# A decoder layer on one core: another order of work in the rows of the first two batches

## The chip, the cores and the metric

The kernel runs on one core of a Trainium2 chip. The time is the device time of one execution in microseconds. The kernel before was run three times: 654.48 us is the median, 654.33 the lowest and 656.54 the highest. One more execution was profiled, and every row below is from it.

## The reference

The layer works on 32 batches of 112 rows of 256 numbers (float32), one batch independent of the next:

```
x = x + attention(layernorm(x), wq, wk, wv, wo)     # 8 heads of 128, rms norm and rotation of q and k, causal softmax
x = x + gelu(layernorm(x) @ ctx^T) @ ctx            # ctx: 375 rows of 256 for each batch
x = x + ffn(layernorm(x), w1, b1, w2, b2)           # 256 -> 1024 -> 256, weights, biases and inputs rounded to fixed point
```

wq, wk, wv and wo are 256 x 1024 in size (1 MB each), w1 and w2 are 1024 x 256 (1 MB each).

## The kernel before, in words

**Precision.** The attention's matrix products run on float16 pairs: a number is rounded to a high half, and the rest goes into a low half. Each product is three matmuls (high x high, high x low, low x high). So xn (the normalised x), q, k, o and the four attention weights are all "rounded" by the Scalar engine (ACT, high half) and then "split" by the Vector engine (DVE, low half = value - high half). The weights are first lifted by a power of two that follows from the sum of their squares: ACT squares, TensorE (PE) sums over partitions (`sum_weights`), DVE bounds the sum (`bound_weights`, L435), GpSimd (POOL) takes the root (`root_weights`, L334), DVE makes the power of two (`lift_weights`, L440), ACT rounds with it as scale, DVE splits.

**Pipeline.** Each engine runs a list of its own: `body(i)` for i from -3 to 36, and in one body it works on different stages of several batches. The order within a body is written out by hand, engine by engine, and semaphores tie the engines together. There is no loop in the hardware: all bodies are unrolled. "The row of batch j" is here the DVE body in which c = j: it begins with `turn_cos_k(j)` (L425: k times cosines, out of PSUM) and `turn_sin_k(j)` (L433), goes on with the sums of squares of k and q (`sum_squares_k` L565, `sum_squares_q` L602), the rotation of q (`turn_cos_q` L568, `turn_sin_q` L605, `turn_q` L612), and ends with `split_k(j)` (L637); `split_q(j)` (L520) is in the body after it. ACT's part of a row is: scale and round k (L769 to L784), round q (L786 to L798), normalise and round o of the batch before, then square k, copy v, square q of the batch after. POOL adds the two halves of k's rotation (`turn_k`, L352) and takes the rms roots (L356, L375).

**One buffer each.** xn16, xT16 (its transposed copy), the q, k and v banks of PSUM, turn_c, turn_s and qk16 have one buffer. So the transposition of batch j's xn (`transpose_x`, a DMA that SP issues, L285) waits for the last v matmul of batch j - 1.

**The start.** Batch 0's xn is made first. Then `prepare_projections` lifts, rounds and splits wk, wq and wv (DVE L468, ACT L721). PE projects k, q and v of batch 0, and between k and q it sums wo's squares. On DVE the row of batch 0 then runs: the statistics of batch 1's x (`stats_x`), then `prepare_wo` (L481): bound, lift and split wo, and only then `turn_cos_k(0)`. Batch 1's x is normalised in the middle of this row, behind `turn_cos_q(0)`, and split behind that. On ACT, `prepare_wo` (L730) squares wo, waits for its lift, rounds it, and then `square_k(0)` follows, which `turn_cos_k(0)` waits for. In the next DVE body, behind `split_q(0)`, stand `clip_weights` of w1 and w2 and `fixed_biases` (L486, L492): they wait for ACT's `round_weights` (L738), which stands between the v copies and `square_q(1)`.

**Queues.** SP issues every DMA in the order of its list: `transpose_x(1)`, then the load of batch 2's x, of w1 and w2 (`load_weights`, L244; they go into the place of the raw projection weights), then the transpositions of k and q of batch 0.

Of the kernel before, what the change touches and what calls it, by code (L numbers as in the profile page):

```python
# [77 lines left out]
def decoder_layer(nc, x, ctx_rows, ctx_cols, wq, wk, wv, wo, w1_cols, b1, w2_cols, b2, tables, out):  # L78
# [15 lines left out]
    with ExitStack() as stack:  # L94
# [225 lines left out]
        @block.gpsimd  # L320
        def _(pool):
            pool.memset(ones_pp[:, :], 1.0).then_inc(const_done, 1)
            pool.memset(nhalf[:, :], -0.5).then_inc(const_done, 1)
            pool.memset(ln_eps[:, :], LN_EPS).then_inc(const_done, 1)
            pool.memset(eps_0[:, :], RMS_EPS / QK_LIFT ** 2).then_inc(const_done, 1)
            pool.memset(v_sb[:, :, D:VW], V_DROP).then_inc(const_done, 1)
            pool.memset(pool_cell[:, :], 0.0).then_inc(const_done, 1)
            pool.wait_ge(const_done, 6)

            def carry_wait():  # L330

                pool.tensor_tensor(pool_cell[:, :], pool_cell[:, :], pool_cell[:, :], ALU.mult)

            def root_weights():  # L334
                for n in TURN:
                    pool.wait_ge(w_sq_done, TURN.index(n) + 1)
                    pool.tensor_tensor(w_root[:, n:n + 1], w_sq[:, n:n + 1], nhalf[:, 0:1], ALU.pow).then_inc(w_root_done, 1)

            def variance_x(j):
                pool.wait_ge(x_stats_done, done(j))  # L340
                pool.tensor_tensor(ve[0][:, :], mv[0][:, 1:2], ln_eps[:, :], ALU.add).then_inc(x_var_done, 1)  # L341

            def add_b2(j):
                if j.has(1):
                    pool.wait_ge(out_done, done(j.plus(-1)))
                pool.tensor_tensor(x3b[:, :], x3[:, :], b2_rows[:, :], ALU.add).then_inc(x3b_done, 1)  # L346

            def root_x(j):
                pool.wait_ge(x_var_done, done(j))
                pool.tensor_tensor(rstd[0][:, :], ve[0][:, :], nhalf[0:T, 0:1], ALU.pow).then_inc(x_rstd_done, 1)  # L350

            def turn_k(j):  # L352
                pool.wait_ge(k_sin_done, done(j))
                pool.tensor_tensor(turn_c[:, 1, :], turn_c[:, 1, :], turn_s[:, 1, :], ALU.add).then_inc(k_turned, 1)  # L354

            def rms_root_k(j):  # L356
                pool.wait_ge(k_summed, done(j))
                if is_first(j):
                    pool.wait_ge(eps_done, TURN.index(1) + 1)
                pool.tensor_tensor(ms[:, 1, :], ss[:, 1, :], rms_eps[:, 1, :], ALU.add).then_inc(k_ms_done, 1)  # L360
                pool.wait_ge(k_ms_done, done(j))
                pool.tensor_tensor(rms[:, 1, :], ms[:, 1, :], nhalf[0:T, 0:H], ALU.pow).then_inc(k_rms_done, 1)  # L362

            def mask_later_keys(j):
                pool.wait_ge(exp_done, done(j))
                carry_wait()
                p = p_sb.rearrange("k (h t) -> k h t", h=H)
                pool.affine_select(out=p, in_=p, compare_op=ALU.is_ge, fill=0.0, base=0,  # L368
                                   pattern=[[0, H], [1, T]], channel_multiplier=-1).then_inc(p_done, 1)

            def root_x3(j):
                pool.wait_ge(x3_stats_done, done(j))
                pool.tensor_tensor(rstd[2][:, :], ve[2][:, :], nhalf[0:T, 0:1], ALU.pow).then_inc(x3_rstd_done, 1)

            def rms_root_q(j):  # L375
                pool.wait_ge(q_summed, done(j))
                if is_first(j):
                    pool.wait_ge(eps_done, TURN.index(0) + 1)
                pool.tensor_tensor(ms[:, 0, :], ss[:, 0, :], rms_eps[:, 0, :], ALU.add).then_inc(q_ms_done, 1)
                pool.wait_ge(q_ms_done, done(j))  # L380
                pool.tensor_tensor(rms[:, 0, :], ms[:, 0, :], nhalf[0:T, 0:H], ALU.pow).then_inc(q_rms_done, 1)  # L381

            def root_x2(j):
                pool.wait_ge(x2_stats_done, done(j))
                pool.tensor_tensor(ve[1][:, :], mv[1][:, 1:2], ln_eps[:, :], ALU.add).then_inc(x2_var_done, 1)  # L385
                pool.wait_ge(x2_var_done, done(j))
                pool.tensor_tensor(rstd[1][:, :], ve[1][:, :], nhalf[0:T, 0:1], ALU.pow).then_inc(x2_rstd_done, 1)

            def body(i):
                a, b, c, d, f, g = (Batch(i + 3), Batch(i + 2), Batch(i + 1), Batch(i - 0), Batch(i - 2), Batch(i - 3))  # L390
                if a.inside(B):
                    variance_x(a)
                if g.inside(B):
                    add_b2(g)
                if a.inside(B):
                    root_x(a)
                    if a.off == 0:
                        root_weights()
                if b.inside(B):
                    turn_k(b)  # L400
                    rms_root_k(b)
                if c.inside(B):
                    mask_later_keys(c)
                if f.inside(B):
                    root_x3(f)
                if b.inside(B):
                    rms_root_q(b)
                if d.inside(B):
                    root_x2(d)

            for i in range(-3, B + 5):
                body(i)
# [3 lines left out]
        def _(dve):  # L416
# [51 lines left out]
            def prepare_projections():  # L468
                one, two, three = TURN[0:3]
                bound_weights(one)  # L470
                bound_weights(two)
                lift_weights(one)
                lift_weights(two)
                split_projection(one)
                bound_weights(three)
                lift_weights(three)
                split_projection(two)
                split_projection(three)
                dve.wait_ge(table_in, 32)

            def prepare_wo():  # L481
                bound_weights(3)
                lift_weights(3)
                split_wo()

            def clip_weights(n):  # L486

# [153 lines left out]
            def body(i):  # L641
# [4 lines left out]
                    stats_x2(f)  # L646
                if d.inside(B):
                    split_q(d)
                    if d.off == 0:
                        clip_weights(0)  # L650
                        clip_weights(1)
                        fixed_biases()
                if f.inside(B):
                    normalise_x2(f)
                if b.inside(B):
                    stats_x(b)
                if i.inside(B):
                    residual_out(i)
                if e.inside(B):
                    split_o(e)  # L660
                if c.inside(B):
                    if c.off == 0:
                        prepare_wo()
                    turn_cos_k(c)
                    turn_sin_k(c)
                if g.inside(B):
                    residual_ctx(g)
                if c.inside(B):
                    sum_squares_k(c)
                    turn_cos_q(c)  # L670
                if b.inside(B):
                    normalise_x(b)
                if g.inside(B):
                    stats_x3(g)
# [1 line left out]
                    gelu_inner(f)  # L676
                if h.inside(B):
                    clip_hidden1(h)
                if b.inside(B):
                    split_xn(b)  # L680
                    if b.off == 0:
                        prepare_projections()
# [13 lines left out]
                if e.inside(B):  # L696
                    residual_attention(e)
                if c.inside(B):
                    split_k(c)

            for i in range(-3, B + 5):
# [4 lines left out]
        def _(act):  # L706
# [20 lines left out]
                round_projection(two)  # L727
                round_projection(three)

            def prepare_wo():  # L730
                act.wait_ge(wo_in, 16)
                for c in range(MC):
                    act.activation(wo16[:, 0, c * HH:(c + 1) * HH, :].bitcast(BF16), wo_raw[:, c * HH:(c + 1) * HH, :], ACT.Square,
                                   scale=W_PEAK, accum_out=w_sum[:, 3, c:c + 1]).then_inc(w_squared, 1)
                act.wait_ge(w_lift_done, 4)
                act.activation(wo16[:, 0, :, :], wo_raw[:, :, :], ACT.Copy, scale=w_lift[:, 3:4]).then_inc(wo_done, 1)

# [108 lines left out]
            def body(i):  # L846
# [2 lines left out]
                    square_h(g)  # L849
                if i.inside(B):  # L850
                    relu0(i)
                if c.inside(B):
                    round_xn(c)
                    if c.off == 0:
                        prepare_projections()
# [13 lines left out]
                    round_o(e)  # L869
                if c.inside(B):  # L870
                    if c.off == 0:
                        prepare_wo()
                    square_k(c)
                if d.inside(B):
                    copy_v1(d)
                    copy_v0(d)
# [2 lines left out]
                        round_weights(1)  # L879
                if c.inside(B):  # L880
                    square_q(c)
                if f.inside(B):
                    copy_xn2T(f)
                if h.inside(B):
# [7 lines left out]
        def _(pe):  # L892
# [47 lines left out]

            def project_k(j):
                pe.wait_ge(xT_landed, landed_once(j))
                if j.has(3):
                    pe.wait_ge(x2_done, done(j.plus(-3)))
                project(1, 0, k_ps[:, 0, :], j)
# [188 lines left out]
```

## Time and profile before

| what | value |
|---|---|
| median of three runs | 654.48 us |
| the profiled execution | 654.7 us, its span 652.9 us |
| DVE busy | 588.1 us (90%) |
| PE busy | 593.3 us (91%) |
| ACT busy | 543.0 us (83%) |
| POOL busy | 348.0 us (53%) |
| mean granted clock of TensorE | 0.974 of full speed |

The span is what the trace covers; the execution's own time is 1.8 us more. Matmuls overlap in the pipeline, so PE's busy time is not a measure of how full PE is. In the chain of work that ended last, 75% of the span is DVE.

### The profile page before, as it was taken

Reading aid. Unit: us, or ns where it says so; the run is one execution under the profiler, and the core shown is the slowest. Engines: PE = TensorE matmul, PEld = TensorE weight load, DVE = VectorE, ACT = ScalarE, POOL = GpSimd, SP = SyncE. Lnnn points to the kernel's source line nnn. Section 1 sums busy time; section 2 is a strip of 40 time slices with the busy share of each in tenths; the row PEclk is TensorE's granted clock in tenths of the full one; section 3 lists DMA queues with packets and bytes.
Section 4 is the critical chain, followed back from the end, with each engine's and each line's share of the span. In section 5 each row is a group of like instructions: output and inputs, shape, how many; then the busy total and the mean of one; then the engine's idle time right before and its main releaser. Section 6 shows DMA issues by size and latency. Waiting matters only on the chain.

```text
span 652.9 us, 13103 instructions
## 1 busy us (share of the span) xinstructions
PE 593.3 (91%) x4624; PEld 477.3 (73%) x4624; DVE 588.1 (90%) x1339; ACT 543.0 (83%) x1402; POOL 348.0 (53%) x430
## 2 busy tenths in 40 slices
PE   1746889999999999999999999999999999997864
PEld 1424667777887788888778877888887788776753
DVE  3768899999999999999999999999999999998442
ACT  6675788999999999989998899999889999998522
POOL 1134555665555565666655555656666555556111
PEclk9967999999999999999999999999999999999978
DMA  8071566766776766667687676666677777666451
GB/s 296 0 200 36 114 139 138 137 138 150 149 148 137 147 133 142 141 141 153 133 151 152 143 152 138 137 142 132 143 149 138 150 152 146 134 141 138 89 109 37
DMA packets 222641, 88.92 MB, mean 136 GB/s; under 512 B 200704, under 2 KB 217552, under 8 KB 222320
## 3 DMA queue, kind: packets, MB, share of 16 engines
q1 hardware_dynamic: 222576, 88.08, 63.6%
q8 instruction: 37, 0.61, 0.4%
q14 instruction: 28, 0.23, 0.1%
HBM read 34.84 MB, written 3.67 MB: 59 GB/s over the span
## 4 chain that ended last, share of the span: by engine, by line
DVE 75%; ACT 9%; PE 5%; POOL 3%; issue 3%; DMA 3%; SPq 0%; ACTq 0%; DVEq 0%
DVE turn_s L433 11%; DVE turn_c L425 8%; DVE qk L524 8%; DVE o L550 5%; DVE ss L566 5%; DVE turn_c L614 5%; DVE ss L603 5%; DVE qk L639 4%; DVE h_t L590 2%; DVE y_out L545 2%; DVE g L628 2%; DVE x L634 2%; DVE stat L534 1%; POOL turn_c L354 1%; DVE xn L600 1%
## 5 line engine op out<-in xcount | busy, mean ns | idle before, releaser
L912 PE MATMUL psum<-wqkv,xT 128*112 128x512 f16 x384 | 148.3, 386 | 12.5 <-DMA xT<-xn 9.1
L913 PE MATMUL psum<-wqkv,xT 128*112 128x512 f16 x384 | 147.4, 384 | 0.0
L914 PE MATMUL psum<-wqkv,xT 128*112 128x512 f16 x384 | 147.1, 383 | 0.0
L354 POOL TENSOR_TENSOR turn_c<-turn_c,turn_s 112x1024 f32<-112x1024 f32 x32 | 75.7, 2365 | 48.4 <-DVE turn_s L433 48.4
L912 PEld LDWEIGHTS psum<-wqkv,xT 128*112 128x112 f16 x384 | 50.7, 132 | 43.4 <-DMA xT<-xn 9.7
L425 DVE TENSOR_TENSOR turn_c<-psum,cos_t 112x1024 f32<-112x1024 f32 x64 | 77.8, 1215 | 0.0
L433 DVE TENSOR_TENSOR turn_s<-psum,sin_t 112x1024 f32<-112x1024 f32 x64 | 77.7, 1214 | 0.0
L914 PEld LDWEIGHTS psum<-wqkv,xT 128*112 128x112 f16 x384 | 50.7, 132 | 34.1 <-issue 1.9
L922 PE MATMUL psum<-wo,oT 128*112 128x256 f16 x256 | 71.0, 277 | 4.7 <-DMA oT<-o 3.5
L524 DVE SCALAR_TENSOR_TENSOR qk<-turn_c,rms,qk 112x128 f16<-112x128 f32 x256 | 69.2, 343 | 2.6 <-ACT qk L796 2.5
L924 PE MATMUL psum<-wo,oT 128*112 128x256 f16 x256 | 71.0, 277 | 0.0
L923 PE MATMUL psum<-wo,oT 128*112 128x256 f16 x256 | 71.0, 277 | 0.0
L913 PEld LDWEIGHTS psum<-wqkv,xT 128*112 128x112 f16 x384 | 50.7, 132 | 27.6 <-issue 1.3
L385 POOL TENSOR_TENSOR ve<-mv,ln_eps 112x1 f32<-112x1 f32 x32 | 6.6, 205 | 109.1 <-DVE mv L518 109.1
L1051 PE MATMUL psum<-v_sb,p_sb 112*112 112x129 f32 x512 | 62.1, 273 | 0.5 <-DVE turn_s L433 0.5
L1051 PEld LDWEIGHTS psum<-v_sb,p_sb 112*112 112x112 f32 x512 | 58.9, 176 | 0.9 <-POOL p_sb L368 0.9
L346 POOL TENSOR_TENSOR x3b<-x,b_rows 112x256 f32<-112x256 f32 x32 | 48.3, 1509 | 16.5 <-DVE y_out L545 13.2
L362 POOL TENSOR_TENSOR rms<-ms,nhalf 112x8 f32<-112x8 f32 x32 | 55.1, 1723 | 2.5
L381 POOL TENSOR_TENSOR rms<-ms,nhalf 112x8 f32<-112x8 f32 x32 | 53.3, 1665 | 2.5
L341 POOL TENSOR_TENSOR ve<-mv,ln_eps 112x1 f32<-112x1 f32 x32 | 9.2, 287 | 81.0 <-DVE mv L537 81.0
L1013 PE MATMUL psum<-qkT 128*112 128x112 f16 x256 | 42.6, 218 | 10.0 <-DVE turn_s L433 9.7
L961 PE MATMUL psum<-ctx_in,g 125*112 125x256 f32 x192 | 48.6, 390 | 3.3 <-ACT v_sb L708 3.3
(107 smaller groups left out, 1699.2 us busy)
## 6 DMA issues: line engine op xcount, KB each, us to landing
ctxT<-in_ctx_cols SPq DMA_DIRECT2D x32, 375.0 KB, 3.4
ctx_in<-in_ctx_rows SPq DMA_DIRECT2D x32, 375.0 KB
x_in<-in_x SPq DMA_DIRECT2D x32, 112.0 KB, 2.3
out_y<-y_out SPq DMA_DIRECT2D x32, 112.0 KB, 2.9
w_raw<-in_w SPq DMA_DIRECT2D x2, 1024.0 KB, 6.1
w_raw<-in_wk SPq DMA_DIRECT2D x2, 512.0 KB, 5.0
w_raw<-in_wq SPq DMA_DIRECT2D x2, 512.0 KB, 6.5
w_raw<-in_wv SPq DMA_DIRECT2D x2, 512.0 KB, 8.2
```

What stands on the lines that cost most here:

```text
L354: pool.tensor_tensor(turn_c[:, 1, :], turn_c[:, 1, :], turn_s[:, 1, :], ALU.add).then_inc(k_turned, 1)
L362: pool.tensor_tensor(rms[:, 1, :], ms[:, 1, :], nhalf[0:T, 0:H], ALU.pow).then_inc(k_rms_done, 1)
L425: return dve.tensor_tensor(turn_c[:, w, :].rearrange("t (b h d) -> t b h d", b=2, d=D), ps.rearrange("t b (h d) -> t b h d", d=D), cos_t[: ...
L433: return dve.tensor_tensor(turn_s[:, w, :].rearrange("t (h two f) -> t h two f", two=2, f=HALF), halves, table, ALU.mult)
L524: last = dve.scalar_tensor_tensor(out=qk16[:, 0, 1, at], in0=turn_c[:, 0, at], scalar=rms[:, 0, h:h + 1], in1=qk16[:, 0, 0, at], op0=ALU.m ...
L912: pe.matmul(dst, hi, wqkv[:, 0, c, w, cols], start=c == 0, stop=False)
L913: pe.matmul(dst, hi, wqkv[:, 1, c, w, cols], start=False, stop=False)
L914: last = pe.matmul(dst, lo, wqkv[:, 0, c, w, cols], start=False, stop=c == MC - 1)
L922: pe.matmul(y_ps, oT16[:, h, :], wo16[:, 0, h, :], start=first and h == heads[0], stop=False)
L923: pe.matmul(y_ps, oT16[:, h, :], wo16[:, 1, h, :], start=False, stop=False)
L924: product = pe.matmul(y_ps, oT16[:, H + h, :], wo16[:, 0, h, :], start=False, stop=last and h == heads[-1])
L1051: last = pe.matmul(o_ps[:, h // OH, at:at + VW], p_sb[:, h * T:(h + 1) * T], v_sb[:, h, :], start=h % OH == 0, stop=h % OH == OH - 1 or h ...
```

## The change

The change moves instructions and adds one wait; no instruction's size or number changes.

- Batch 1's x: `stats_x(1)` goes behind the first split of `prepare_projections`, `normalise_x(1)` to its end; `split_xn(1)` goes behind `turn_sin_k(0)`. POOL's `variance_x(1)` and `root_x(1)` go between the second and the third of the weight roots. ACT's `round_xn(1)` goes behind `square_k(0)`.
- wo: DVE's `bound_weights(3)` goes to the end of `prepare_projections`, `lift_weights(3)` between `turn_cos_k(0)` and `turn_sin_k(0)`, and `split_wo` ahead of `split_k(0)`. ACT's rounding of wo goes behind `square_q(0)`.
- The feed-forward weights: `clip_weights` of w1 and w2 and `fixed_biases` go from behind `split_q(0)` to ahead of `split_k(1)`.
- PE's `project_k(1)` waits for `turn_sin_k(0)` by itself, since xn's order no longer implies it.

```diff
@@ POOL @@
             def body(i):
+                early = a.off == 1
-                if a.inside(B):
+                if a.inside(B) and not early:
                     variance_x(a)
...
-                if a.inside(B):
+                if a.inside(B) and not early:
                     root_x(a)
                     if a.off == 0:
-                        root_weights()
+                        root_weights(TURN[0:2])
+                        variance_x(Batch(1))
+                        root_x(Batch(1))
+                        root_weights(TURN[2:])
...
@@ DVE, prepare_projections @@
                 lift_weights(two)
                 split_projection(one)
+                stats_x(Batch(1))
                 bound_weights(three)
                 lift_weights(three)
                 split_projection(two)
                 split_projection(three)
+                normalise_x(Batch(1))
+                bound_weights(3)
                 dve.wait_ge(table_in, 32)
-
-            def prepare_wo():
-                bound_weights(3)
-                lift_weights(3)
-                split_wo()
...
@@ DVE, body @@
                 if d.inside(B):
                     split_q(d)
-                    if d.off == 0:
-                        clip_weights(0)
-                        clip_weights(1)
-                        fixed_biases()
...
-                if b.inside(B):
+                if b.inside(B) and b.off != 1:
                     stats_x(b)
...
                 if c.inside(B):
+                    turn_cos_k(c)
                     if c.off == 0:
-                        prepare_wo()
-                    turn_cos_k(c)
+                        lift_weights(3)
                     turn_sin_k(c)
+                    if c.off == 0:
+                        split_xn(Batch(1))
...
-                if b.inside(B):
+                if b.inside(B) and b.off != 1:
                     normalise_x(b)
...
-                if b.inside(B):
+                if b.inside(B) and b.off != 1:
                     split_xn(b)
...
                 if c.inside(B):
+                    if c.off == 0:
+                        split_wo()
+                    if c.off == 1:
+                        clip_weights(0)
+                        clip_weights(1)
+                        fixed_biases()
                     split_k(c)
...
@@ ACT @@
-            def prepare_wo():
+            def square_wo():
                 act.wait_ge(wo_in, 16)
...
+            def round_wo():
                 act.wait_ge(w_lift_done, 4)
...
-                if c.inside(B):
+                if c.inside(B) and c.off != 1:
                     round_xn(c)
...
                     if c.off == 0:
-                        prepare_wo()
+                        square_wo()
                     square_k(c)
+                    if c.off == 0:
+                        round_xn(Batch(1))
...
                     square_q(c)
+                    if c.off == 0:
+                        round_wo()
...
@@ PE @@
             def project_k(j):
                 pe.wait_ge(xT_landed, landed_once(j))
+                if j.off == 1:
+                    pe.wait_ge(k_sin_done, done(j.plus(-1)))
```

## Rows read from the trace of the kernel before

**Rows 1.** Busy us in one stretch: PE, PEld, DVE, ACT, POOL; PEclk, DMA share, GB/s
```profile
101.70:585.00 483.30, 482.40 (x3864) 391.84 (x3863) 478.62 (x1102) 437.48 (x1154) 291.35 (x351) 1.00 0.69 143
```

**Rows 2.** The chain that ended last: start us, us, what
```profile
24.95 2.01 ACT wo L736
27.06 2.35 DVE wo L461
...
35.50 2.37 DMA xT<-xn
```

**Rows 3.** Timeline of DVE to 51 us: start, us, line, operation [idle before <-releaser]
```profile
17.62 0.16 DVE L438 TENSOR_SCALAR w_sq<-psum 128x1 f32<-128x1 f32 x1 [1.77 <-PE psum L902]
...
23.42 0.42 DVE L534 BATCH_NORM_STATS2 stat<-x_in 112x6 f32<-112x256 f32 x1
...
29.65 1.21 DVE L425 TENSOR_TENSOR turn_c<-psum,cos_t 112x1024 f32<-112x1024 f32 x1
30.77 1.22 DVE L433 TENSOR_TENSOR turn_s<-psum,sin_t 112x1024 f32<-112x1024 f32 x1
...
37.77 1.23 DVE L614 TENSOR_TENSOR turn_c<-turn_c,turn_s 112x1024 f32<-112x1024 f32 x1
...
42.30 2.19 DVE L524 SCALAR_TENSOR_TENSOR qk<-turn_c,rms,qk 112x128 f16<-112x128 f32 x8 [1.11 <-ACT qk L796]
...
48.60 0.69 DVE L418 TENSOR_SCALAR w2T<-w_int 128x2048 bf16<-128x2048 int16 x1 [1.10 <-ACT w_int L741]
...
50.28 0.42 DVE L534 BATCH_NORM_STATS2 stat<-x_in 112x6 f32<-112x256 f32 x1
...
50.84 1.19 DVE L425 TENSOR_TENSOR turn_c<-psum,cos_t 112x1024 f32<-112x1024 f32 x1
```

**Rows 4.** Timeline of ACT, 22 to 64 us
```profile
22.71 0.19 ACT L733 ACTIVATION_READ_ACCUMULATOR wo<-wo_raw 128x1 f32 x1
...
42.97 1.02 ACT L819 ACTIVATE sq<-psum 112x1024 f32<-112x1024 f32 x1 [0.70 <-PE psum L914]
...
44.85 3.72 ACT L741 ACTIVATE w_int<-w_raw 128x2048 int16<-128x2048 f32 x2
48.45 1.03 ACT L830 ACTIVATE sq<-psum 112x1024 f32<-112x1024 f32 x1
...
57.57 1.28 ACT L772 ACTIVATE kn<-turn_c,rms 112x128 f32<-112x128 f32 x4 [0.57 <-POOL rms L362]
...
63.35 1.10 ACT L803 ACTIVATE on<-psum,rden 112x128 f32<-112x128 f32 x4
```

**Rows 5.** Timeline of PE, 23 to 39 us
```profile
23.04 0.58 PE L902 MATMUL psum<-w_sum,ones_pp 128*128 128x1 f32 x4 [0.59 <-ACT wo L733]
...
28.46 0.38 PE L914 MATMUL psum<-wqkv,xT 128*112 128x512 f16 x1
37.91 0.68 PE L912 MATMUL psum<-wqkv,xT 128*112 128x512 f16 x1 [9.07 <-DMA xT<-xn]
```

**Rows 6.** Timeline of POOL, 36 to 39 us
```profile
36.97 1.65 POOL L381 TENSOR_TENSOR rms<-ms,nhalf 112x8 f32<-112x8 f32 x1
```

**Rows 7.** Issues of line L236 (the load of batch 1's x): issue time and landing
```profile
L236 SPq DMA_DIRECT2D x_in<-in_x x1: 484/484/484, 4.4 to 4.4; - x1
...
DMA to landing us min/median/max: 8.8/8.8/8.8
```

**Rows 8.** Timeline of DVE in batch 1's row, 54 to 68 us
```profile
54.20 1.22 DVE L425 TENSOR_TENSOR turn_c<-psum,cos_t 112x1024 f32<-112x1024 f32 x1
...
61.13 1.23 DVE L639 TENSOR_TENSOR qk<-kn,qk 112x1024 f16<-112x1024 f32 x1 [0.96 <-ACT qk L708]
62.28 0.23 DVE L509 RECIPROCAL rden<-psum 112x6 f32<-112x6 f32 x2
...
67.76 1.21 DVE L425 TENSOR_TENSOR turn_c<-psum,cos_t 112x1024 f32<-112x1024 f32 x1
```

**Rows 9.** Issues of line L275 (q's transposition) to 50 us: time to landing
```profile
DMA to landing us min/median/max: 4.7/4.7/4.7
```

More of the change, by code:

```diff
@@ L332, in carry_wait, with root_weights @@
                 pool.tensor_tensor(pool_cell[:, :], pool_cell[:, :], pool_cell[:, :], ALU.mult)
-            def root_weights():
-                for n in TURN:
+            def root_weights(turns):
+                for n in turns:
                     pool.wait_ge(w_sq_done, TURN.index(n) + 1)
```

## The prediction

> **What bounds the kernel now.** I read the busy time by stretch first. From 102 to 585 us the DVE is busy for 478.62 of 483.30 us [rows 1], 99%, and there each batch costs what its DVE work costs. Nothing in that stretch is edited. So I looked for when the stretch can begin, with the chain of waits: at the start the chain runs through ACT's rounding of wo (24.95, 2.01 us), DVE's split of wo (27.06, 2.35 us), and later through the transposition of batch 1's xn (35.50, 2.37 us) [rows 2]. All three stand in the row of batch 0, and all are moved. The timelines of the engines then give the dates: the reader is to see that `turn_cos_k` of batch 0 starts at 29.65, of batch 1 at 50.84 [rows 3], of batch 2 at 67.76 [rows 8]. If batch 2's start comes earlier by some time, everything behind it (same order, same waits, each on something in these rows or later) comes earlier by the same time. So the sum is made for this one date, 67.76, and subtracted from the end.
>
> The trace is of an execution of 654.7 us with a span of 652.9; the median of the runs is 654.48, 0.2 lower.
>
> **Batch 1's statistics, at no cost.** `stats_x(1)` takes 50.84 - 50.28 = 0.56 us [rows 3]. It goes ahead of the third weight bound, before which DVE idles 1.77 us, from 15.85 to 17.62, waiting for PE [rows 3]. x of batch 1 is there by 4.4 + 8.8 = 13.2 (or half a us more, if the landing counts from the issue's end) [rows 7]. POOL's two small operations behind it fit ahead of the third root too, since 1.2 us of that idle time are left. If the cover were gone, 0.56 us would push the v weights and through them only the v projection, which is late for nothing here.
>
> **Start of batch 0's row: 29.65 becomes 24.0.** PE was done with k of batch 0 at 23.04 - 0.59 = 22.45, for it waited that long for ACT's squares of wo [rows 5]. ACT ends these squares at 22.71 + 0.19 = 22.90 [rows 4] as before, and `square_k(0)`, now next, takes 1.02 [rows 4]: 23.92. On DVE, `normalise_x(1)` takes the place of the statistics at 23.42 (some 0.42, until 23.85); the sum of wo's squares is there at 23.04 + 0.58 = 23.62 [rows 5], and the bound takes 0.16. So `turn_cos_k(0)` starts at 24.0, earlier by 5.65.
>
> **The lift inside the rotation: 0.2.** ACT began to round wo at 24.95 [rows 2], right behind the lift, so the root was there by 24.8, and its bound is no later now; DVE gets to the lift at 24.0 + 1.12 = 25.12 and does not wait. One operation like the bound and the wait for its own result: 0.2. `turn_sin_k(0)` starts at 25.3, before at 30.77 [rows 3].
>
> **To `split_q(0)`: 42.30 becomes 36.85.** Between `turn_sin_k(0)` and `split_q(0)` lay 42.30 - 30.77 = 11.53 us, and the latter waited for ACT (1.11 idle) [rows 3]: POOL's rotation and roots, ACT's scaling and rounding. None of that chain is edited, so 25.3 + 11.53 = 36.85, if nothing else is late:
> - DVE: the six operations from `turn_sin_k(0)` to `turn_q(0)` take 1.12 each (30.77 - 29.65), `split_xn(1)` 0.4: done at 32.5. (Before, 8.23 from 30.77 to the end of `turn_q` at 37.77 + 1.23 [rows 3], with the normalising and splitting of xn and a wait in it; by that figure 33.5.) `split_wo` with its two small followers took 29.65 - 27.06 = 2.6 [rows 2, 3]: 35.1 (36.1). Then `split_k(0)`, one step of 1.15 (62.28 - 61.13 [rows 8]): 36.25 (37.25). So it hides, or costs 0.4 by the other figure. I take 0.
> - ACT: q of batch 0 is projected by about 26.3 (PE finishes the v behind it at 28.46 + 0.38 = 28.84 [rows 5], 24 matmuls later); `round_xn(1)` and `square_q(0)` follow, then the rounding of wo (2.01) until some 29.3. k's scaling is wanted at about 31, so the rounding is in ACT's idle time and wo is there long before `split_wo`.
>
> **The transposition of xn(1): off the path.** The low half is done at about 26.9, so what holds it is the last v matmul at 28.84: it starts there, not at 35.50, and lands at 31.2 where PE started k of batch 1 at 37.91 [rows 5]. In the trace k took from there to 42.97 - 0.02 (ACT waited 0.70 for it [rows 4]), 5.0 us, with the first matmul 0.68 us long and the last of batch 0's 0.38 [rows 5]. With the same 5.0, k is there at 36.3, and ACT is free for `square_k(1)` at 36.8. The added wait of `project_k(1)` is over at 26.5, before the transposition lands; what queues behind it on PE (q, scores, v) is not held by it.
>
> **Start of batch 1's row: 50.84 becomes 39.5.** Behind `split_q(0)` (some 2.1 to the next instruction's start) stood the clips and biases until 50.28 [rows 3]: 50.28 - 42.30 - 2.1 = 5.9 us, mostly waits for ACT's rounding of w1 and w2. They leave. 36.85 + 2.1 + 0.56 = 39.5, a gain of 11.3. x of batch 2 and the squares of k (36.8 + 1.02) are there.
>
> **Inside batch 1's row: 0.9 is given back.** ACT's piece from `square_k(1)` (42.97) to the end of `square_q(1)` (48.45 + 1.03), with the rounding of w1 and w2 in it, takes 6.5 [rows 4]. It now runs from 36.8 to 43.3. DVE is ready for `turn_cos_q(1)` at 39.5 + 3 x 1.12 = 42.85, so it waits 0.45. w1 and w2 land in time: their loads stand behind the transposition, which moves by 6.6; ACT took them without a wait at 44.85 and in the middle of 3.72 [rows 4], so they are there by 38.2 and 40.1, and are wanted at 38.7 and 40.5.
> From `turn_cos_q(1)` to where DVE had nothing left took 61.13 - 0.96 - 54.20 = 5.97 [rows 8]: 49.3. Now the clips and biases: the second clip and the biases took 50.28 - 48.60 = 1.68 [rows 3], another clip 0.6: 2.3, until 51.6. `split_k(1)`, which k's rounding would allow at 39.5 + 1.12 + 61.13 - 50.84 - 1.12 = 49.8, starts at 51.6; the reciprocals of the softmax sums follow 1.15 later and take 0.23 [rows 8]: 53.0. They release ACT's normalising of o, which by its own queue could start at 39.5 + 63.35 - 50.84 = 52.0. So the clips hold it by 1.0. From there to `turn_cos_k(2)` it was 67.76 - 63.35 = 4.41 [rows 4, 8]: 57.4.
>
> **Sum.** 67.76 - 57.4 = 10.4. 654.7 - 10.4 = 644.3; against the median 644.1, which I take. Between 11.3 and 10.4 lies what batch 1's row gives back.
>
> One place where a rule speaks against the change: in the trace POOL's power for q's rms runs from 36.97 for 1.65 us [rows 6], and DVE's `turn_q`, with two inputs in SBUF, runs in it at 37.77 with its usual 1.23 [rows 3]: neither is held up. The Trainium skill says otherwise (SBUF — State Buffer, "Who interferes with whom"): a DVE instruction with two SBUF inputs and a POOL instruction that reads SBUF lock each other out for a whole instruction. By that rule `split_xn(1)`, which now starts as POOL's rotation of k does, would hold POOL or be held; rival C has the sum.
>
> **Rivals.**
> A. The forecast, 60%: 643.3 to 645.2 by the roundings of the steps.
> B. Row 1 gives back more, 17%. The scores of batch 0 stand behind q's transposition and behind `turn_sin_k(1)`, their exponentials ahead of k's scaling on ACT. Before, the latter wait ended last, at 50.84 + 1.12 + 1.22 = 53.2, 2.35 behind `turn_cos_k(1)`, and ACT still had 0.57 us idle ahead of the scaling [rows 4]. q's transposition landed 4.7 after its issue [rows 9]; from 39.05 that is 43.75 now, 4.25 behind `turn_cos_k(1)`. So the scaling would be 4.25 - 2.35 - 0.57 = 1.3 late, of which the clips' hold hides 1.0. Every us more goes through whole: a landing after twice 4.7 gives 5.0 in all, 649.1. For it: the 2 MB of w1 and w2 come in ahead on the same queue. Against: they come 2 us earlier, relative to the transposition, than before, so 4.7 should be the upper end.
> C. The lock, 6%. If POOL's rotation of k starts first, `split_xn(1)` waits its 2.4 us; k's sums come 1.45 late for the rms, `split_wo` ends at 37.5 and `split_k(0)` at 38.65, so `split_q(0)` is 1.8 late; the clips then weigh less, and `turn_cos_k(2)` comes at 58.8: 645.5. If DVE is first, 644.4.
> D. More gain, 7%: neither `square_q(1)` nor the clips hold the row, 11.7 in all: 642.8.
> E. Nothing at the end, 6%: the long stretch is held by something that these rows don't start (PE is as busy there as DVE, 482.40 of 483.30 [rows 1]). 654.5. Against it: PE's list, too, follows from the same rows.
> F. Slower, 4%: w1 lands so late that ACT's rounding, which stands ahead of `square_q(1)` and so ahead of all of batch 1's q, holds the row. It takes the whole gain away from 38.7 + 10.4 + 0.5 = 49.6 on, 21 us behind the transposition at 28.84, where it took at most 44.85 - 35.50 = 9.4; at 55 it would be 660. Against it: nothing but the transpositions shares the queue.
>
> **How the numbers follow.** 644.1 is A's time. 642.4 to 648.5 holds A, C, D and most of B, some 87%; what is left out is E, F and the tail of B, and some allowance for what I don't see. Faster by over 0.5% (3.3 us, about what can be told from no change) is A to D: 0.90. Within 0.5%: E, 0.06. Slower: F, 0.04.
>
> **What would show it.** In the trace after: `turn_cos_k(0)` at 24.0; the transposition of xn(1) right behind the last v matmul of batch 0, at 28.9; `split_q(0)` at 36.9; `turn_cos_k(1)` at 39.5 with no clip ahead of it; DVE waiting 0.4 for ACT's `square_q` ahead of `turn_cos_q(1)`; `split_k(1)` right behind the biases, with no idle time; `turn_cos_k(2)` at 57.4; and from there every date 10.4 earlier. Wrong would be a wait of ACT for w1's load, DVE idle ahead of `split_wo`, a late k(1) on PE, or dates that drift back behind batch 2.

## The result, and the profile after

645.43 us, the median of four runs (643.96 to 648.09), against 654.40 for the kernel before on the same chip, now the median of four runs as well: a ratio of 0.986, 95% interval 0.984 to 0.9881. The forecast was 644.1, in a range of 642.4 to 648.5. Direction and mechanism came out, but one step of the sum failed. The profiled execution hides that at first sight: its span is 10.7 us shorter than before, but of these only 8.8 are there when the last batch's row starts.

The head of the page after:

```profile
span 642.2 us, 13103 instructions
PE 593.6 (92%) x4624; PEld 477.1 (74%) x4624; DVE 587.8 (92%) x1339; ACT 543.5 (85%) x1402; POOL 350.5 (55%) x430
```

DVE's timeline after (line numbers moved by 4: L429 is turn_cos, L437 turn_sin, L526 split_q, L422 a clip):

```profile
23.54 1.22 DVE L429 TENSOR_TENSOR turn_c<-psum,cos_t 112x1024 f32<-112x1024 f32 x1
...
24.86 1.23 DVE L437 TENSOR_TENSOR turn_s<-psum,sin_t 112x1024 f32<-112x1024 f32 x1
26.00 0.41 DVE L602 TENSOR_TENSOR xn<-xn 112x256 f16<-112x256 f32 x1
...
36.47 2.19 DVE L526 SCALAR_TENSOR_TENSOR qk<-turn_c,rms,qk 112x128 f16<-112x128 f32 x8 [0.58 <-ACT qk L804]
...
39.14 1.19 DVE L429 TENSOR_TENSOR turn_c<-psum,cos_t 112x1024 f32<-112x1024 f32 x1
...
42.85 1.23 DVE L429 TENSOR_TENSOR turn_c<-psum,cos_t 112x1024 f32<-112x1024 f32 x1 [0.27 <-ACT sq L838]
...
47.60 1.47 DVE L616 TENSOR_TENSOR turn_c<-turn_c,turn_s 112x1024 f32<-112x1024 f32 x1
48.99 0.68 DVE L422 TENSOR_SCALAR w1T<-w_int 128x2048 bf16<-128x2048 int16 x1
49.59 0.68 DVE L422 TENSOR_SCALAR w2T<-w_int 128x2048 bf16<-128x2048 int16 x1
...
51.28 1.22 DVE L641 TENSOR_TENSOR qk<-kn,qk 112x1024 f16<-112x1024 f32 x1
52.41 0.23 DVE L511 RECIPROCAL rden<-psum 112x6 f32<-112x6 f32 x2
54.63 2.19 DVE L526 SCALAR_TENSOR_TENSOR qk<-turn_c,rms,qk 112x128 f16<-112x128 f32 x8 [1.98 <-ACT qk L804]
...
58.91 1.21 DVE L429 TENSOR_TENSOR turn_c<-psum,cos_t 112x1024 f32<-112x1024 f32 x1
```

The reader is to see three things. The rows of the first two batches start as forecast: 23.54 (24.0), 39.14 (39.5), against 29.65 and 50.84 [rows 3]; this execution began its weights 0.37 earlier, and with that added the second date is 39.51. The clips run in one go behind `turn_q(1)`. But behind the reciprocals stands a wait of 1.98 for ACT that the forecast did not have, and batch 2's row starts at 58.91 (59.28 with the 0.37 added), not 57.4.

PE after: the first matmul of k of batch 1, the first of the scores of batch 0:

```profile
30.98 0.42 PE L924 MATMUL psum<-wqkv,xT 128*112 128x512 f16 x1 [2.50 <-DMA xT<-xn]
...
43.34 0.34 PE L1027 MATMUL psum<-qkT 128*112 128x112 f16 x1 [5.29 <-DMA qkT<-qk]
```

k of batch 1 starts at 30.98 instead of 37.91 [rows 5]. The scores now wait for q's transposition, 4.6 us from issue to landing, as rival B had it, and no longer for `turn_sin_k(1)`.

POOL and ACT after, in batch 1's row, tell where the 1.98 comes from:

```profile
47.00 0.98 POOL L368 TENSOR_SCALAR_AFFINE_SELECT p_sb<-p_sb 112x896 f32<-112x896 f32 x1
47.96 2.38 POOL L379 TENSOR_TENSOR ms<-ss,rms_eps 112x8 f32<-112x8 f32 x1
50.42 1.64 POOL L381 TENSOR_TENSOR rms<-ms,nhalf 112x8 f32<-112x8 f32 x1
```

```profile
49.15 1.06 ACT L714 ACTIVATE qk<-kn 112x1024 f16<-112x1024 f32 x1
52.15 1.28 ACT L798 ACTIVATE qk<-turn_c,rms 112x128 f16<-112x128 f32 x4 [1.95 <-POOL rms L381]
53.33 1.26 ACT L804 ACTIVATE qk<-turn_c,rms 112x128 f16<-112x128 f32 x4
54.50 1.11 ACT L811 ACTIVATE on<-psum,rden 112x128 f32<-112x128 f32 x4
```

The addition ahead of q's roots, 8 numbers a row, took 2.38 us; in the kernel before, the same instruction took 0.194 on the mean, and in batch 1's row:

```profile
58.60 0.19 POOL L379 TENSOR_TENSOR ms<-ss,rms_eps 112x8 f32<-112x8 f32 x1
```

In the changed kernel it ends at 50.34, just when DVE's second clip does (49.59 + 0.68 = 50.27). The roots, ACT's rounding of q, `split_q(1)` and the normalising of o follow it, each late. And DVE's `turn_q`, 1.47 us instead of 1.23, ends late beside the mask (47.00 to 47.98).

### The profile page after: what moved, and what is told of

Its sections match the earlier page's. It is cut to its first block, busy times and chain, and to the rows that moved or that the text cites. A ratio compares the mean times of both kernels' runs of the same rounds, so it can differ in the third digit from the quotient of the medians.

```text
span 642.2 us, 13103 instructions
## 1 busy us (share of the span) xinstructions
PE 593.6 (92%) x4624; PEld 477.1 (74%) x4624; DVE 587.8 (92%) x1339; ACT 543.5 (85%) x1402; POOL 350.5 (55%) x430
## 4 chain that ended last, share of the span: by engine, by line
DVE 74%; ACT 8%; PE 6%; issue 4%; POOL 4%; DMA 3%; SPq 0%; ACTq 0%; POOLq 0%
DVE turn_s L437 10%; DVE qk L526 9%; DVE turn_c L429 8%; DVE o L552 5%; DVE turn_c L616 5%; DVE ss L605 5%; DVE ss L568 5%; DVE qk L641 4%; DVE h_t L592 2%; DVE y_out L547 2%; DVE g L630 2%; DVE x L636 2%; DVE stat L583 1%; DVE xn L602 1%; DVE x L565 1%
## 5 line engine op out<-in xcount | busy, mean ns | idle before, releaser
L429 DVE TENSOR_TENSOR turn_c<-psum,cos_t 112x1024 f32<-112x1024 f32 x64 | 77.8, 1215 | 0.3 <-ACT sq L838 0.3
L437 DVE TENSOR_TENSOR turn_s<-psum,sin_t 112x1024 f32<-112x1024 f32 x64 | 77.7, 1215 | 0.0
L526 DVE SCALAR_TENSOR_TENSOR qk<-turn_c,rms,qk 112x128 f16<-112x128 f32 x256 | 69.1, 343 | 2.7 <-ACT qk L804 2.7
L1015 PE MATMUL psum<-xn2T,ctxT 128*125 128x112 f32 x384 | 48.8, 277 | 1.7 <-ACT xn2T L714 1.6
L975 PE MATMUL psum<-ctx_in,g 125*112 125x256 f32 x192 | 46.8, 380 | 3.3 <-ACT v_sb L714 3.3
```

The costliest lines, as they stand in the source:

```text
L429: return dve.tensor_tensor(turn_c[:, w, :].rearrange("t (b h d) -> t b h d", b=2, d=D), ps.rearrange("t b (h d) -> t b h d", d=D), cos_t[: ...
L437: return dve.tensor_tensor(turn_s[:, w, :].rearrange("t (h two f) -> t h two f", two=2, f=HALF), halves, table, ALU.mult)
L526: last = dve.scalar_tensor_tensor(out=qk16[:, 0, 1, at], in0=turn_c[:, 0, at], scalar=rms[:, 0, h:h + 1], in1=qk16[:, 0, 0, at], op0=ALU.m ...
```

## The experiments

Dates of different executions are compared from DVE's first split of wk on (12.6 to 13.5 us into the span). In the table: `turn_sin_k` of batches 1, 2, 4 and 31 so counted, and what is left from the last of these to the end of the span.

| kernel | k(1) | k(2) | k(4) | k(31) | rest |
|---|---|---|---|---|---|
| before | 38.58 | 55.52 | 89.40 | 573.10 | 66.4 |
| changed | 27.24 | 47.05 | 81.33 | 564.66 | 64.5 |
| changed, again | 27.25 | 47.65 | 81.52 | 564.75 | 67.0 |
| undo_wo | 32.68 | 52.41 | 86.66 | 570.12 | 66.5 |
| undo_clips | 32.28 | 49.22 | 83.07 | 566.15 | 66.6 |
| undo_xn | 27.86 | 46.46 | 80.77 | 563.90 | 67.6 |
| clips_in_row2 | 27.25 | 45.87 | 80.66 | 563.88 | 68.9 |
| clips_late_and_rounding_late | 27.26 | 45.84 | 80.61 | 563.83 | 65.1 |
| reduce_in_place_of_clips | 27.24 | 45.84 | 80.62 | 564.62 | 69.0 |
| mask_behind_q_roots | 27.24 | 45.97 | 80.28 | 563.35 | 65.2 |
| both_moved | 27.24 | 44.93 | 78.79 | 561.88 | 64.0 |

The forecast's date for k(2) was 57.4 + 1.12 - 13.37 = 45.2. The last column is the drain behind the last row; it goes from 64.0 to 69.0 over these executions. It makes up all of the 2.5 us between the two profiled spans of the changed kernel (642.2 and 644.7). So steps of 1 us are read from the dates, and the times are given beside them.

**The changed kernel again.** 

> The changed kernel once more, beside its variants. Theory (its gain is the earlier start of batch 2's row and nothing else): turn_cos_k(2) within 0.5 us of 58.9, every later row 8.4 to 8.9 ahead of the kernel before, and 8.5 to 9.5 us less in the median; what a single execution shows beyond that (10.7 in the profiled span) comes behind the last row and changes from run to run. Rival (the tail is shortened by the change): the span is 10 us or more shorter again, with 2 us of it behind the last row.

646.36 us (644.91 to 647.73) beside 654.06: ratio 0.9879 (0.9856 to 0.9901), 7.7 less, a little under what was expected. `turn_cos_k(2)` came at 59.46, 0.06 later than the latest that was expected, the last row 8.35 ahead on the common count, the rest of the span 67.0. The 2 us that the first profiled execution had won in the drain are not the change's. That k(2) is 0.6 later than in the first execution has a cause in these rows: q's transposition took 5.2 us to land, not 4.6, so the scores, the exponentials and POOL's mask came 0.6 later, and the mask (47.55 to 48.53) began together with `turn_q`:

```profile
47.54 2.07 DVE L616 TENSOR_TENSOR turn_c<-turn_c,turn_s 112x1024 f32<-112x1024 f32 x1
```

`turn_q` took 2.07 us where it took 1.47 in the first execution and takes 1.23 alone.

**Clips in batch 2's row.** 

> The clips and biases go from ahead of split_k(1) to batch 2's row, ahead of residual_attention(0), where DVE waited 1.45 us for PE. Theory L (in batch 1's row the two clips held GpSimd's addition for q's rms, 2.38 instead of 0.20 us, and through it ACT's rounding of q, 1.95 of wait, and split_q(1), 1.98 of wait): the addition takes 0.2 again, ACT rounds q right behind k, split_q(1) starts at 52.6, turn_cos_k(2) at 57.0 instead of 58.9. The clips' 2.3 us in batch 2's row cost 0 to 0.9, so rows from batch 4 on are 1.0 to 1.9 earlier, and the time 1 to 2 us less than the changed kernel's. Rival V (it is the clips' DVE time ahead of split_k(1), 2.3 us, not GpSimd): the same dates at batch 2, so this run alone does not part them; the next one does. Rival N (neither matters, q is late for another reason): turn_cos_k(2) stays at 58.9.

```diff
                     if c.off == 1:
-                        clip_weights(0)
-                        clip_weights(1)
-                        fixed_biases()
                     split_k(c)
...
+                if c.off == 2:
+                    clip_weights(0); clip_weights(1); fixed_biases()
                 if e.inside(B):
                     residual_attention(e)
```

Batch 2's row starts 1.2 to 1.8 earlier, and 0.5 to 0.9 of that is lost again by batch 4: 0.7 to 0.9 is left there, less than the 1.0 to 1.9 expected. 646.33 us (643.41 to 647.19), the same as the changed kernel's. POOL and then DVE in this run:

```profile
47.63 1.16 POOL L379 TENSOR_TENSOR ms<-ss,rms_eps 112x8 f32<-112x8 f32 x1
...
65.42 2.63 POOL L381 TENSOR_TENSOR rms<-ms,nhalf 112x8 f32<-112x8 f32 x1
```

```profile
47.23 1.51 DVE L616 TENSOR_TENSOR turn_c<-turn_c,turn_s 112x1024 f32<-112x1024 f32 x1
...
66.64 0.69 DVE L422 TENSOR_SCALAR w1T<-w_int 128x2048 bf16<-128x2048 int16 x1
67.24 0.69 DVE L422 TENSOR_SCALAR w2T<-w_int 128x2048 bf16<-128x2048 int16 x1
```

The addition is not back at 0.2: it still ends with `turn_q` (47.23 + 1.51 = 48.74), which has two inputs in SBUF. And in batch 2's row the clips now hold the end of POOL's roots: 2.63 instead of 1.64, until 68.05, where the clips end at 67.93. The expectation had missed both.

**Two row sums in place of the clips.** 

> As clips_in_row2, but in the old place of the clips stand two extra row sums over 112x1024 (2.25 us of DVE time, one input, results unused). Theory L (GpSimd was held by the kind of operation): GpSimd's addition stays at 0.2, ACT rounds q without the 1.95 wait; split_k(1) is as late as in the changed kernel (51.2), the softmax reciprocals release ACT at 52.9 and turn_cos_k(2) comes at 57.3. Rival V (DVE's time): turn_cos_k(2) at 58.9 as in the changed kernel.

```diff
                     if c.off == 1:
-                        clip_weights(0); clip_weights(1); fixed_biases()
+                        dve.tensor_reduce(spare[:, 0, :], heads(sq[:, 0, :]), AX_X, ALU.add)
+                        dve.tensor_reduce(spare[:, 1, :], heads(sq[:, 1, :]), AX_X, ALU.add)
                     split_k(c)
```

DVE and POOL:

```profile
48.85 1.21 DVE L707 TENSOR_REDUCE spare<-sq 112x8 f32<-112x1024 f32 x1
49.98 1.20 DVE L708 TENSOR_REDUCE spare<-sq 112x8 f32<-112x1024 f32 x1
51.11 1.21 DVE L642 TENSOR_TENSOR qk<-kn,qk 112x1024 f16<-112x1024 f32 x1
```

```profile
47.83 1.16 POOL L380 TENSOR_TENSOR ms<-ss,rms_eps 112x8 f32<-112x8 f32 x1
49.07 1.64 POOL L382 TENSOR_TENSOR rms<-ms,nhalf 112x8 f32<-112x8 f32 x1
```

DVE is as busy ahead of `split_k(1)` as with the clips, and k(2) stands at 45.84, as in clips_in_row2. The addition takes 1.16, not the 0.2 expected, for `turn_q` holds it here too. So behind a q that is late by that much, DVE's time ahead of `split_k(1)` doesn't hold the row, and rival V falls as the reason for the late row of the changed kernel: what the clips cost there they cost through POOL, 1.2 us (1.8 against the second execution). That this time of DVE is free in every case is not shown; undo_xn below has a case where it is not. This kernel was run once, 648.23 us, and nothing is read from that time.

**w1 and w2 rounded later as well.** 

> As clips_in_row2, and ACT rounds w1 and w2 behind square_q(1) instead of ahead of it. Theory: DVE's wait of 0.27 ahead of turn_cos_q(1) goes, square_q(1) starts at 38.2 instead of 41.8, and the 3.7 us of rounding end at 42.9, before ACT is wanted for xn of batch 2 (43.7): turn_cos_k(2) up to 0.3 earlier than in clips_in_row2, 56.7. Rival (q of batch 1 is not there at 38.2, or the exponentials are pushed): no gain or up to 0.5 lost.

```diff
-                    if d.off == 0:
-                        round_weights(0); round_weights(1)    # ahead of square_q(1)
...
                     square_q(c)
+                    if c.off == 1:
+                        round_weights(0); round_weights(1)
```

DVE's wait of 0.27 is gone, and k(2) is no earlier (45.84): k's scaling on ACT stands behind the exponentials, and these wait for the scores. No gain, no loss in the rows; 644.28 us (643.21 to 647.12), not parted from clips_in_row2.

**The parts undone one by one.** Each of the three is the reverse of one item of the change.

> The changed kernel with the clips and biases back behind split_q(0). Theory: w1 and w2 still come 6.6 us earlier than in the kernel before, so ACT has rounded them by 41.9; DVE waits for that and turn_cos_k(1) starts at 43.8 instead of 39.1; then batch 1's row runs unhindered, 16.9 long, and turn_cos_k(2) comes at 60.7 instead of 58.9: this part of the change is worth some 2 us, not the 5.9 that left batch 0's row. Rival (the wait for ACT's rounding was worth its whole 5.9): turn_cos_k(2) at 64 or later.

```diff
                     split_q(d)
+                    if d.off == 0:
+                        clip_weights(0); clip_weights(1); fixed_biases()
...
-                    if c.off == 1:
-                        clip_weights(0); clip_weights(1); fixed_biases()
                     split_k(c)
```

> The changed kernel with wo bounded, lifted, rounded and split ahead of turn_cos_k(0) as before. Theory (wo's preparation stood on the path): turn_cos_k(0) at 29.3 instead of 23.5, and all behind it 5.5 later, turn_cos_k(2) at 64.4, some 5.5 us more in the time. Rival (batch 0's row has slack, what counts is batch 1's xn): turn_cos_k(2) less than 2 us later.

```diff
+                    if c.off == 0:
+                        bound_weights(3); lift_weights(3); split_wo()
                     turn_cos_k(c)
-                    if c.off == 0:
-                        lift_weights(3)
...
                         square_wo()
+                        round_wo()
                     square_k(c)
```

> The changed kernel with batch 1's statistics, normalising, rounding and splitting back in batch 0's row (behind turn_cos_q(0)). Theory (off the path as soon as wo and the clips are moved): the transposition of xn(1) starts at 29.5 to 30 instead of 28.6, DVE waits 0.5 to 1 for ACT's half, turn_cos_k(1) at most 0.5 later, turn_cos_k(2) 0 to 0.5 later. Rival (the transposition of xn(1), which stood in the chain of waits before, is what the change gains by): batch 1's k comes late, and turn_cos_k(2) is over 2 us later.

```diff
-                stats_x(Batch(1))
-                normalise_x(Batch(1))
...
-                    if c.off == 0:
-                        split_xn(Batch(1))
...
-                if b.inside(B) and b.off != 1:
+                if b.inside(B):
                     stats_x(b)      # normalise_x, split_xn, POOL's and ACT's likewise
```

The first two came out near the dates expected. With the clips back, `turn_cos_k(1)` was at 43.83 and `turn_cos_k(2)` at 60.73, in an execution that began 0.35 earlier than the changed kernel's, so 0.4 late on the common count. With wo back, `turn_cos_k(2)` was at 64.75 in an execution that began 0.47 later, so 0.1 early. DVE with the clips back, then with wo back:

```profile
39.79 0.69 DVE L422 TENSOR_SCALAR w1T<-w_int 128x2048 bf16<-128x2048 int16 x1 [1.48 <-ACT w_int L749]
41.59 0.69 DVE L422 TENSOR_SCALAR w2T<-w_int 128x2048 bf16<-128x2048 int16 x1 [1.10 <-ACT w_int L749]
...
43.83 1.19 DVE L429 TENSOR_TENSOR turn_c<-psum,cos_t 112x1024 f32<-112x1024 f32 x1
```

```profile
27.08 2.35 DVE L465 SCALAR_TENSOR_TENSOR wo<-wo_raw,w_lift,wo 128x2048 f16<-128x2048 f32 x1 [2.14 <-ACT wo L743]
...
29.67 1.20 DVE L429 TENSOR_TENSOR turn_c<-psum,cos_t 112x1024 f32<-112x1024 f32 x1
```

wo's move is worth 5.3 us at k(4), the clips' 1.7. In time: 651.07 (649.58 to 651.91), ratio to before 0.9945 (0.9928 to 0.9962), and 646.97 (646.59 to 647.34), ratio 0.9888 (0.9864 to 0.9912); by the times alone the second is not parted from the changed kernel. xn's move, beside the other two, is worth less than nothing in this profile: without it k(1) comes 0.6 later, and k(2) 0.6 to 1.2 earlier, not 0 to 0.5 later; 646.30 us (646.03 to 647.70), not parted by time either. The three don't add up to the 8.1 us that the change wins at k(4) (5.3 + 1.7 - 0.6 = 6.4): the rest is won by more than one of them, and undoing one alone does not lose it. For undo_xn, POOL, DVE and ACT say why k(2) is earlier:

```profile
48.12 0.19 POOL L379 TENSOR_TENSOR ms<-ss,rms_eps 112x8 f32<-112x8 f32 x1
48.38 1.64 POOL L381 TENSOR_TENSOR rms<-ms,nhalf 112x8 f32<-112x8 f32 x1
```

```profile
44.14 1.22 DVE L426 TENSOR_TENSOR turn_c<-psum,cos_t 112x1024 f32<-112x1024 f32 x1 [1.12 <-ACT sq L831]
...
50.03 0.69 DVE L419 TENSOR_SCALAR w1T<-w_int 128x2048 bf16<-128x2048 int16 x1
```

```profile
53.71 1.14 ACT L804 ACTIVATE on<-psum,rden 112x128 f32<-112x128 f32 x4 [1.02 <-DVE rden L506]
```

DVE waits 1.12 for q's squares and comes to `turn_q` (48.89) and the clips that much later. The addition is over by then, 0.19 long; `turn_q` runs over the end of the roots, and neither is longer for it (1.23 and 1.64); the clips begin as the roots end (50.02). A stall that was removed had kept two engines apart. With q on time, ACT now waits 1.02 for the reciprocals, which stand behind the clips: here the clips do cost DVE's time.

**The mask behind q's roots.** 

> The changed kernel, where GpSimd masks batch 0's scores behind the two rms operations for batch 1's q, not ahead of them; clips and biases stay in batch 1's row. Theory L (an operation of GpSimd and one of DVE on the shared access hold each other only if they meet: the addition for q's rms met the clips because it stood behind the mask, which waits for the scores, and these for the transposition of q): the addition now runs at 46.5, ahead of turn_q and the clips, in 0.2; ACT rounds q right behind k; turn_q takes 1.23 again instead of 1.47. The mask meets turn_q and the clips instead and may be held up to 50.0, so the weighing of values ends by 53 and turn_cos_k(2) comes at 57.8 or earlier, against 58.9. Rival (whatever GpSimd runs there is held, and the row waits for it all the same): turn_cos_k(2) at 58.9 or later.

```diff
-                if c.inside(B):
+                if c.inside(B) and c.off != 0:
                     mask_later_keys(c)
...
                 if b.inside(B):
                     rms_root_q(b)
+                if c.off == 0:
+                    mask_later_keys(c)
```

POOL, then DVE:

```profile
46.76 0.20 POOL L379 TENSOR_TENSOR ms<-ss,rms_eps 112x8 f32<-112x8 f32 x1 [0.61 <-DVE ss L607]
47.04 1.64 POOL L381 TENSOR_TENSOR rms<-ms,nhalf 112x8 f32<-112x8 f32 x1
48.64 1.69 POOL L332 TENSOR_TENSOR pool_cell<-pool_cell 1x1 f32<-1x1 f32 x1
50.29 0.98 POOL L368 TENSOR_SCALAR_AFFINE_SELECT p_sb<-p_sb 112x896 f32<-112x896 f32 x1
```

```profile
47.85 1.23 DVE L618 TENSOR_TENSOR turn_c<-turn_c,turn_s 112x1024 f32<-112x1024 f32 x1
...
50.19 1.10 DVE L498 TENSOR_SCALAR b_int<-b_raw 128x8 int16<-128x8 f32 x1
```

As theory L has it: the addition takes 0.20, `turn_q` 1.23, and now the mask's little forerunner is held, 1.69 us for one number, until the clips end at 50.28; the mask in its turn holds a bias operation, 1.10 for 0.17. k(2) is 1.1 to 1.7 earlier. ACT again waits for the reciprocals, 0.82 us. 643.88 us (642.02 to 644.48), ratio to before 0.984 (0.9819 to 0.986), with the clips where the change put them; the interval touches the changed kernel's.

**Both, each clip in a place of its own.** 

> The version that the runs point to: the mask behind q's roots as in mask_behind_q_roots; w1 and w2 rounded behind square_q(1); w1's clip between residual_attention(0) and split_k(2), w2's ahead of split_q(2), the biases' rounding ahead of split_q(0) and the rest of the biases ahead of split_k(1), all places where DVE was idle for about as long and where the theory expects GpSimd not to hold them. Theory: counted from the first split of wk, turn_sin_k(2) at 45.1 (46 in the variants with late clips, 47 to 47.6 in the changed kernel) and turn_sin_k(4) at 79.3 (80.6 and 81.3 to 81.5), so some 2 us less than the changed kernel in the time. Rival (the places' idle time is needed, each clip costs its own 0.6 where it stands): turn_sin_k(4) at 80.5, no better than clips_in_row2.

```diff
                 if d.inside(B):
+                    # ahead of it: round_biases() if d.off == 0, clip_weights(1) if d.off == 2
                     split_q(d)
...
                     residual_attention(e)
+                if c.off == 2:
+                    clip_weights(0)
...
                     if c.off == 1:
-                        clip_weights(0); clip_weights(1); fixed_biases()
+                        clip_biases()
                     split_k(c)
```

DVE in batch 2's row of this version:

```profile
66.59 0.48 DVE L640 SCALAR_TENSOR_TENSOR x<-psum,y_unit,x_in 112x256 f32<-112x256 f32 x1
66.98 0.68 DVE L424 TENSOR_SCALAR w1T<-w_int 128x2048 bf16<-128x2048 int16 x1
67.64 1.22 DVE L645 TENSOR_TENSOR qk<-kn,qk 112x1024 f16<-112x1024 f32 x1
...
69.47 0.66 DVE L424 TENSOR_SCALAR w2T<-w_int 128x2048 bf16<-128x2048 int16 x1
```

k(2) at 44.93, k(4) at 78.79, both earlier than expected: at k(4) 2.5 to 2.7 us before the changed kernel's rows, and 10.6 before the kernel before's. GpSimd and DVE still meet, against the expectation: the two clips of the biases take 1.29 us beside the mask, 0.37 elsewhere, and the mask's forerunner 0.48 instead of 0.18 beside `turn_q`. But the reciprocals then wait for PE (0.36), so nothing on the path waits for these two. 643.08 us (641.22 to 644.82), ratio 0.9837 (0.9815 to 0.986). By the dates it is the best of all; by the times alone it is not parted from the changed kernel (0.986, 0.984 to 0.9881).

## Why the prediction was right, and where it was wrong

- Right, to 0.1 us: the start of both rows and what they rest on. On the common count `turn_sin_k(1)` was forecast at 39.5 + 1.12 - 13.37 = 27.25 and measured at 27.24 in the profile after. Undoing wo's move gives 5.4 back at k(1), what it was priced at (5.65 less 0.2 for the lift). The clips' move takes 5.0 us out at k(1), where the sum had 5.9 with the earlier rounding in it, and keeps 1.7 of them at k(4).
- Wrong: "Inside batch 1's row: 0.9 is given back". It was 2.9: of the 11.3 at k(1), 8.5 are left at k(2) (7.9 in the second execution). The step that failed is q's way to ACT: the sum let the normalising of o wait for the reciprocals alone, and took POOL's addition and roots for q, and ACT's rounding of q behind them, as no later than before. In its place ACT waited 1.95 for POOL, behind an addition of 2.38 us instead of 0.19. Of the 2.9, 0.8 is rival B's chain: ACT's scaling of k starts 6.44 us behind `turn_sin_k(1)`, before 5.62, and both_moved still gives 0.75 back. The other 2.1 is about what the addition took longer (2.2). The price of the clips' DVE time did not fail: in undo_xn, where the addition takes 0.19, the clips and biases take 2.28 (2.3 in the sum) and hold ACT by 1.02 (1.0 in the sum); in the changed kernel this is hidden behind the late q. The forecast's date for k(2), 45.2, is reached in both_moved (44.93), where the mask, the clips of w1 and w2 and their rounding have left q's way.
- Wrong: the passage on the rule, which left the lock to rival C and to `split_xn(1)` alone. The Trainium skill's rule (SBUF — State Buffer, "Who interferes with whom") is what happened, in another place than the one that I weighed. It names DVE operations with two SBUF inputs, and some with one input that run in a fast mode, and POOL operations. In these runs a `turn_q` (two inputs) and the clips (one input, 2048 numbers of a partition in 0.68 us, where a row sum takes 1.21 for 1024) held additions and the mask's forerunner, and the mask held `turn_q` (1.41 to 2.07). Two row sums beside the roots and over their end held nothing (1.64). I had let one pair decide, the power for q's roots with `turn_q` inside it [rows 3, 6], which run side by side here too, against the rule as the page has it; it was the wrong witness. With clips at its end it is held as well (2.63), with `turn_q` at its end it is not. Why is not shown; that most of its time is neither reading nor writing would be one reading. At `split_xn(1)`, where rival C saw it, it cost 0.1: POOL's rotation of k took 2.47 instead of 2.36.
- Missed: POOL's mask stands ahead of q's roots. So the late scores (rival B's chain) did not only reach ACT, they moved the addition onto the clips. That the mask's place matters is shown by moving it.
- In size, luck helped: the rows show 8.4 less, and 10.4 was forecast; the median of the first four runs is 9.0 less, that of the second set 7.7. The room that the range had above the forecast was made for a late landing (rival B), and most of what filled it was POOL's addition, for which the sum had nothing.

A witness that was to be had in the trace of before, and that the profile after repeats at the start of the rows of batches 3 and 4: POOL's small addition for x's variance, 0.19 us when alone, beside DVE's split of o. POOL, then DVE, after:

```profile
92.08 1.25 POOL L341 TENSOR_TENSOR ve<-mv,ln_eps 112x1 f32<-112x1 f32 x1 [2.39 <-DVE mv L539]
```

```profile
92.06 1.22 DVE L552 TENSOR_TENSOR o<-on,o 112x1024 f16<-112x1024 f32 x1
```

Open: between k(2) and k(4) the changed kernel loses 0.4 against before (34.28 and 33.88). In that stretch PE's clock was granted at 0.86 on the mean where it was 1.00 before. From 62 to 66 us it was near the lower of its two levels, 1.2 of 2.4 GHz (0.56 and 0.59 in two stretches of 2 us), behind 2 us in which PE was busy for 0.60. First after, then before:

```profile
58.00:70.00 12.00, 10.08 (x72) 7.51 (x71) 10.04 (x11) 8.07 (x19) 7.40 (x8) 0.86 0.50 91
```

```profile
67.00:79.00 12.00, 10.08 (x86) 8.05 (x84) 10.91 (x12) 8.06 (x19) 7.25 (x8) 1.00 0.59 123
```

In the same stretch DVE waited 1.45 for the output projection. But the second execution had the same 0.86 and lost nothing there, so this is not shown.

## What to carry to other kernels

When a group of operations is moved, ask not only whether DVE has the time there, but what GpSimd does at that moment: a short operation of GpSimd beside a long one of DVE, and the other way round, can last as long as the other, and what waits for it moves by the whole. A duration that differs from the same instruction's elsewhere is the sign, and the trace has it as a group's mean above its minimum (for the small addition of the trace of before, 0.287 and 0.191). And a stall that an edit removes may be what kept two engines apart.

## What the runs showed that I had not expected

One number of work on GpSimd took 1.69 us beside two clips; a power of 1.64 us was unmoved by a `turn_q` in its middle or over its end, and 1.0 longer with clips at its end. And the drain behind the last row varies from 64.0 to 69.0 us over these executions, and by 2.5 between two of the same kernel.
